# VectorE's loop turned so that it begins with a step's closing multiply, one product moved from step 0 to step 3, one transpose moved to the front of step 7

## What is computed

```python
x = x + L0(x, cond)   # attention over two keys: a fixed one and one made of cond
x = x + L1(x, cond)   # gated MLP, plus 8 experts with the top 2 chosen by a router
x = x + L2(cond, x)   # x @ W_e plus a row made of cond
x = x + L3(x, h0=cond)

def step(carry, xz_t):                      # L3, one position
    prev_h, prev_c = carry
    z = xz_t + prev_h @ Wh                  # 4 gates of 256, for 2 sequences
    ai, af, ao, ag = jnp.split(z, 4, axis=1)
    next_c = sigmoid(af) * prev_c + sigmoid(ai) * tanh(ag)
    next_h = sigmoid(ao) * tanh(next_c)
```

## Time and profile before

| | |
|---|---|
| median of 3 runs | 2004.42 us (2003.37 to 2004.9) |
| profiled execution | 2006.19 us, of it 2004.4 us span |
| TensorE busy | 1848.3 us (92%) |
| weight loads busy | 1462.6 us (73%) |
| VectorE busy | 1351.8 us (67%) |
| GpSimd busy | 1134.2 us (57%) |
| ScalarE busy | 812.2 us (41%) |
| DMA | 14.67 MB, mean 7 GB/s |

### The profile page before, as it was taken

One profiled execution on the slowest core, in us unless ns is written; L12 is line 12 of the kernel. 1 busy time (PEld: TensorE's weight loads), 2 busy tenths in 40 slices (PEclk: granted clock), 3 DMA queues, 4 the chain that ended last, 5 costly groups with the idle time before them and its releaser, 6 DMA issues. The chain is left out here.

```text
span 2004.4 us, 255266 instructions
## 1 busy us (share of the span) xinstructions
PE 1848.3 (92%) x113164; PEld 1462.6 (73%) x113164; DVE 1351.8 (67%) x7215; ACT 812.2 (41%) x4757; POOL 1134.2 (57%) x4950
## 2 busy tenths in 40 slices
PE   7899999999999999999999999999999999999998
PEld 5677777777777777777777777777777777777776
DVE  2566666666666666666666666666666666676666
ACT  2344444444444444444444444444444444444443
POOL 3555555555555555555555555555555555555555
PEclk9899999999999999999999999999999999999999
DMA  4000000000000000000000000000000000000000
GB/s 166 3 4 3 3 4 3 3 3 4 3 3 4 3 3 3 4 3 3 4 3 3 4 3 3 3 4 3 3 4 3 3 3 4 3 3 4 3 3 3
DMA packets 57724, 14.67 MB, mean 7 GB/s; under 512 B 56176, under 2 KB 56304, under 8 KB 57200
## 3 DMA queue, kind: packets, MB, share of 16 engines
q1 hardware_dynamic: 57712, 14.50, 3.1%
HBM read 12.37 MB, written 2.10 MB: 7 GB/s over the span
## 5 line engine op out<-in xcount | busy, mean ns | idle before, releaser
L916 PEld LDWEIGHTS psum<-wh_sb,h_ring 128*2 128x2 f32 (+1 forms) x32768 | 519.6, 90 | 446.0 <-DVE h_ring L740 414.9
L916 PE MATMUL psum<-wh_sb,h_ring 128*2 128x64 f32 (+1 forms) x32768 | 690.8, 219 | 138.7 <-DVE h_ring L740 121.4
L926 PE MATMUL psum<-h_ring,wh_sb 128*32 128x2 f32 x65536 | 768.7, 173 | 3.5 <-issue 3.5
L926 PEld LDWEIGHTS psum<-h_ring,wh_sb 128*32 128x32 f32 x65536 | 725.0, 109 | 13.3 <-issue 3.7
L517 ACT ACTIVATE f_act<-psum 128x4 f32<-128x4 f32 x1024 | 177.2, 173 | 763.7 <-DVE psum L711 755.1
L711 DVE STREAM_TRANSPOSE psum<-psum 128x64 f32<-128x64 f32 x1024 | 264.6, 258 | 306.6 <-PE psum L916 306.4
L789 PE MATMUL psum<-up_sb,x 128*32 128x512 f32 x2064 | 282.7, 605 | 0.0
L713 DVE STREAM_TRANSPOSE psum<-psum 128x64 f32<-128x64 f32 x1024 | 270.6, 264 | 16.1 <-PE psum L916 3.0
L795 PE MATMUL psum<-down_e,hid_t 128*16 128x256 f32 x3096 | 268.0, 381 | 0.6 <-ACT down_e L498 0.6
L723 DVE TENSOR_TENSOR_SCAN psum<-addend,psum 128x16 f32<-128x16 f32 x1024 | 199.2, 195 | 71.4 <-ACT psum L520 29.3
L740 DVE SCALAR_TENSOR_TENSOR h_ring<-o_act,psum 128x4 f32<-128x4 f32 x1024 | 163.0, 159 | 116.8 <-ACT psum L526 87.7
(11 more groups left out here) (141 smaller groups left out, 2224.7 us busy)
## 6 DMA issues: line engine op xcount, KB each, us to landing
x_a<-in_x SPq DMA_DIRECT2D x129, 16.0 KB, 1.6
x_s<-in_x SPq DMA_DIRECT2D x129, 16.0 KB, 1.7
up_sb<-in_up SPq DMA_DIRECT2D x1, 2048.0 KB, 12.6
out_y<-y_sb SPq DMA_DIRECT2D x128, 16.0 KB, 1.4
down_sb<-in_down SPq DMA_DIRECT2D x1, 1536.0 KB, 8.2
wx_sb<-in_wx SPq DMA_DIRECT2D x1, 1024.0 KB, 14.7
wh_sb<-in_wh SPq DMA_DIRECT2D x1, 1024.0 KB, 17.9
wkv_sb<-in_wkv SPq DMA_DIRECT2D x1, 512.0 KB, 4.2
```

Source lines behind the costliest of these rows:

```text
L916: last = nc.tensor.matmul(z[32 * j:32 * j + row + B, :], h_ring[:, prev, c, WIN - B - row:WIN], wh_v[:, c, g, j, :], start=False, stop=(c ...
L926: last = nc.tensor.matmul(by_row(z)[32 * j:32 * (j + 1), m, row:row + B], wh_v[:, c, g, j, 32 * m:32 * (m + 1)], h_ring[:, prev, c, WIN - ...
```

## The change

Three edits. First, VectorE's loop is turned by one instruction: the multiply that closes a step now stands at the start of the next step's code, so the close of step 7 is the first instruction of the next turn, behind the loop's branch, and the last close stands behind the loop. So that the first turn has something to close, `o_act` is set to 0 and `c_tanh` to 2 x cond ahead of the loop, which replaces the instruction that wrote the first hidden state. Second, `stream_mm(x1)` goes from step 0 to step 3 of the turn before, behind `attend`, and carries the count `x3_made` (its first instance stands ahead of the loop). Third, the transpose of `hid_s` in step 7 goes from behind the scan to ahead of the f transpose, with its wait for L598's result.

```diff
--- before.py
+++ after.py
@@ -543,10 +543,10 @@
             nc.vector.memset(partial_b, 0.0).then_inc(bank_clear, 1)
             nc.vector.memset(cell_all, 0.0).then_inc(bank_clear, 1)
             nc.vector.memset(addend[:, :], 1.0).then_inc(terms_set, 1)
+            nc.vector.memset(o_act[:, :], 0.0).then_inc(terms_set, 1)
 
             dve.wait_ge(cleared, 11)
             dve.wait_ge(small_in, 16)
-            nc.vector.tensor_scalar(h_ring[:, U - 1, :, WIN - B:WIN], cond, 2.0, None, ALU.mult).then_inc(hid, 1)
             dve.wait_ge(kv_made, 1)
             nc.vector.tensor_tensor(kv[:, :, :], bank[0][:, 0:2 * C * B].rearrange("p (m b) -> p m b", b=B),
                                     b_kv.unsqueeze(2).to_broadcast([P, 2 * C, B]), ALU.add).then_inc(kv_out, 1)
@@ -666,10 +666,13 @@
             hidden_a(2 * U)
             hidden_s(2 * U)
             dve.wait_ge(fold_out, BLOCKS)
-            dve.wait_ge(terms_set, 1)
+            dve.wait_ge(terms_set, 2)
             nc.vector.memset(factor, 0.0).then_inc(terms_set, 1)
-            dve.wait_ge(terms_set, 2)
+            dve.wait_ge(terms_set, 3)
             nc.vector.memset(factor_q[:, :, 3], 0.5).then_inc(terms_set, 1)
+
+            nc.vector.tensor_scalar(c_tanh.rearrange("p (c b) -> p c b", b=B), cond, 2.0, None,
+                                    ALU.mult).then_inc(terms_set, 1)
             dve.wait_ge(bias_scaled, 1)
             bias_x(READY)
             dve.wait_ge(x3_made, READY)
@@ -680,10 +683,24 @@
             invert_inv(2 * U)
             dve.wait_ge(x_injected, READY)
             base_f(READY + U)
-            dve.wait_ge(terms_set, 3)
+            dve.wait_ge(terms_set, 5)
+
+            def close(slot):
+
+                nc.vector.scalar_tensor_tensor(out=h_ring[:, slot, :, WIN - B:WIN],
+                                               in0=o_act[:, :].rearrange("p (c b) -> p c b", b=B), scalar=1.0,
+                                               in1=c_tanh.rearrange("p (c b) -> p c b", b=B),
+                                               op0=ALU.add, op1=ALU.mult).then_inc(hid, 1)
+
 
             with dve.Fori(READY, READY + T, U) as t:
+                now = t
                 for u in range(U):
+                    dve.wait_ge(cell_tanh, now)
+                    if u == 1:
+
+                        dve.wait_ge(h_read, now)
+                    close((u - 1) % U)
                     now = dve.snap(t + (u + 1))
                     if u == 0:
 
@@ -707,6 +724,8 @@
                     elif u == 7:
                         hidden_s(now)
                         invert_inv(now)
+                        dve.wait_ge(hid_s_out, now)
+                        turn(0, hid_s[:, :], hid_st, U)
                     dve.wait_ge(f_made, now)
                     nc.vector.transpose(t_f, z_f).then_inc(f_turned, 1)
                     dve.wait_ge(i_made, now)
@@ -730,17 +749,8 @@
                         bias_x(U)
                     elif u == 6:
                         hidden_a(now)
-                    elif u == 7:
-                        dve.wait_ge(hid_s_out, now)
-                        turn(0, hid_s[:, :], hid_st, U)
-                    dve.wait_ge(cell_tanh, now)
-                    if u == 0:
-
-                        dve.wait_ge(h_read, now)
-                    nc.vector.scalar_tensor_tensor(out=h_ring[:, u, :, WIN - B:WIN],
-                                                   in0=o_act[:, :].rearrange("p (c b) -> p c b", b=B), scalar=1.0,
-                                                   in1=c_tanh.rearrange("p (c b) -> p c b", b=B),
-                                                   op0=ALU.add, op1=ALU.mult).then_inc(hid, 1)
+            dve.wait_ge(cell_tanh, READY + T)
+            close(U - 1)
 
         @block.tensor
         def _(pe):
@@ -908,6 +918,7 @@
             inject().then_inc(x_injected, READY)
             pe.wait_ge(own_first, 2)
             attend(attn_b, w1_own[:, :])
+            stream_mm(x1)
             pe.wait_ge(wh_scaled, 2)
 
             def recur_row(z, g, row, prev):
@@ -947,7 +958,6 @@
                     if u == 0:
 
                         pe.wait_ge(hid_st, now)
-                        stream_mm(x1)
                         down_mm(0).then_inc(stream_made, U)
                     elif u == 1:
 
@@ -965,7 +975,8 @@
                         sum_mm()
                         pe.wait_ge(own_out, now)
 
-                        attend(attn_b, w1_own[:, :]).then_inc(x3_made, U)
+                        attend(attn_b, w1_own[:, :])
+                        stream_mm(x1).then_inc(x3_made, U)
                     elif u == 4:
                         up_mm(0, x1)
                     elif u == 5:
```

## The result

The changed kernel takes 1959.68 us (median of 4 runs, 1959.43 to 1960.97), the kernel before 2004.66 us (4 runs, 2003.37 to 2005.9): a ratio of 0.9777, 95% interval 0.976 to 0.9794.

What follows compares the result with a forecast made beforehand. Bound: the ring of waits in one recurrence step, not an engine. 0.20 + 0.10 - 0.02 - 0.01 = 0.27 us a turn, 34.6 over 128 turns, less 0.4, gives 1970.2 us; own range 1960 to 1980, 8 in 10 1959 to 1987.

Steps and rivals of the forecast that it cites:

- The loop turned: Step 0: the copy for the i gate starts 0.20 us earlier, gaining 0.20 us a turn, ends 0.14 and 0.24.
- The branch behind the scan: End of step 7: the wait for the cell's tanh covers the branch, cost 0, upper bound 0.05 us.
- The stream product out of step 0: Step 1: shorter fillers free the overwriting of x1 earlier, gaining 0.10 us a turn, ends 0.11 and 0.04.
- The stream product into step 3: Steps 3 and 4: TensorE's idle time covers the product, but L604 starts later; cost 0.02 us, ends 0 and 0.10.
- The rival with the passes one behind the other: Steps 3 and 4: the stream products run serially, delaying L604; net 0.16 us a turn slower, 2024 us, chance 0.03.
- The transpose in step 7: Step 7: hid_s's transpose ahead of the f transpose costs 0.01 us, ends 0 and 0.07.
- Ahead of the loop and in its first turns: Ahead of the loop: new instructions, with a multiply and a branch, cost 0.4 us once.
- The clock: TensorE: its clock should stay at the upper level because its idle stretches only get shorter.
- Slower, by the branch: Loop's branch, VectorE: the target must be loaded before the closing multiply, 1.2 us net a turn, about 2160 us, chance 0.02.

Runs made afterwards that it cites:

- e1: The kernel before with the loop turned and the transpose of hid_s moved, the stream product left in step 0: 1973.66 us.
- e5: The changed kernel with one more, long-met wait in front of the copy for the i gate in step 0: 1961.61 us.
- e3: The kernel before with only the transpose of hid_s moved ahead of step 7's f transpose: 2005.11 us.
- e4: The changed kernel with the transpose of hid_s put back behind the scan in step 7: 1966.36 us.
- e9: e2 with the stream product computed a second time in step 7, where it is not needed: 1991.98 us.
- e6: The changed kernel with the stream product computed twice in a row in step 3: 2005.78 us.
- e2: The kernel before with only the stream product moved from step 0 to step 3: 2066.5 us.
- e8: The changed kernel with the stream product in step 7 instead of step 3 and the up products spread over steps 3, 4 and 5: 2631.54 us.
- e11: The changed kernel with the stream product in step 7 instead of step 3 and attend's 8 small products computed again in step 7: 2130.55 us.
- e10: The changed kernel with the stream product in step 7, the first up product split over steps 3 and 4, the second whole in step 5: 1953.54 us.

## Why the prediction was right, and where it was off

The mechanism was right in each term of the sum; the sizes were off in one direction, by 11 us in all. What was said of the clock was wrong, and there the forecast was lucky.

- *The loop turned.* Forecast 0.20 with an upper end of 0.24; measured 0.24 (2.063 to 1.821, and 1.824 in e1). The step that was mis-sized is "the copy for the i gate follows the close directly, at 0.16 (its duration)". It follows at 0.075. So the last spread starts at 0.37 instead of 0.46, the c products at 0.65 instead of 0.74, and L520 at 1.21 instead of 1.25, where the i transpose sets it. The branch's real cost was 0.28 (0.36 less 0.075), and the 0.20 of idle time before the copy showed only the part beyond the close's end. This makes 0.04 a turn, 5 us, and is the largest of the errors. I guessed that e5 would explain the 0.075 by a missing wait, and it did not.
- *The branch behind the scan.* Taken at 0, measured at 0. That the third edit is what makes room for it is shown by the pair e3 and e4: nothing by itself, 5 to 7 us once the branch stands there. The prediction named no worth for it ("removed behind the scan it frees nothing"), which is true of the loop before and false of the turned one.
- *The stream product out of step 0.* Forecast 0.10, measured 0.108 (e9: the same).
- *The stream product into step 3.* I took 0.02 for L604 at 0.52; it came at 0.41 and cost nothing. About half of that is the start: the product began at -0.31 (1008.74 against the close at 1009.05), where I had it at -0.25. The other half is the time from there to L604, 0.72 instead of 0.77. Why it is shorter here than in step 0, where L588 starts 0.80 behind the first filler (1002.92 to 1003.72), is not shown. The rival with the passes one behind the other wanted 1.20 for it and is out. e6 shows that the cover I described as thin is real: past it, 0.43 us of chain cost 0.35.
- *The transpose in step 7.* 0.01 taken, 0.00 measured, partly by luck: I had the transpose of `hid_s` start at 0.50 and overlooked the reciprocal L585 in front of it. It started at 0.56 and left VectorE later than the f product came (the f transpose starts at 0.80), and nothing was lost only because the f transpose then took 0.22 instead of 0.27.
- *Ahead of the loop and in its first turns.* 0.4 us of loss taken; the span less 128 times 0.353 leaves 1.6 us won. That is no gain of the change: the first product of the recurrence starts anywhere from 41.1 to 42.9 us in the profiled executions of this study, at 42.2 before and at 41.2 after.
- *The clock.* "Its idle stretches only get shorter" was wrong as a reason. The second edit leaves TensorE idler around the turn's head: 0.81 us instead of 0.66 from the close of step 6 to the close of step 1, the difference in step 1, and 0.26 us fewer of weight loads in step 0. e2 fell to half its clock in one turn of five for that, 72 us. In the changed kernel the turned loop shortens the same stretch by 0.24 us and the clock stays at 1.00; that the one is the reason of the other is not shown, since 0.79 us of idle time are left there. So the second edit is worth 14 us behind the first (1973.7 to 1959.7) and costs 60 without it. No rival of mine had this, and the forecast was right here by luck: the edits came together, and its argument did not need that. The page "TensorE: Matmul & The Clock Gate" of the Trainium skill (Part 1) has the rule that the clock is set by how busy TensorE has been of late, with half of it when it was too idle; e2 and e9 agree with it (0.50 in one turn of five, and 1.00 once step 7 has work), and the changed kernel beside e2 is not explained by it from the records.
- *Slower, by the branch.* VectorE's branch never had to load code: the changed kernel has 9 packets of it, as the kernel before. But the mechanism exists in this kernel on the engine with the longest turn: e8 and e11. The page "Runtime: NRT & Kernel Launch" of the Trainium skill (Instruction fetch mechanics) has it that a taken branch whose target is not among the stored pages waits until that page is loaded; the trace agrees, with 352 and 135 packets of code against 9, and the long gaps at the loop's head.

## What to carry to other kernels

In a recurrence, read the time from one closing instruction to the next for each step of the loop: the steps that are longer than the shortest one name what can be won (read all of them: step 3 was left out here), and the loop's own branch is one of the things that belongs where an engine waits anyway. Before a filler is moved, compare its chain on the busiest column group with the idle time in its new place, since one chain fitted here for nothing and a second one cost 80% of its length. And check two things that no step's critical path shows: what the work left behind does to TensorE's clock, and whether the turn's code still fits, because the one turned an improvement of single steps into a loss of 60 us (e2), the other into one of 670 us (e8).

## What the runs showed of the hardware that was not expected

- Work that is not needed made a kernel 75 us faster (e2 to e9) by keeping TensorE's granted clock at 2.4 GHz. The clock had fallen with no gap on TensorE longer than 0.64 us ahead of it.
- TensorE's loop with 16 more matmul and 16 more weight-load records in a turn of 882 each loads program code again and again, but not in every turn (135 and 352 packets instead of 9, in 14 and 38 of the turns, gaps up to 5.5 us). With 8 more of each (e10) it does not.
- On VectorE a copy or transpose started 0.075 us behind the start of a 0.16 us multiply, before its end, and others at 0.167; a wait in between that was long met cost 0.004 (0.075 to 0.079, e5).
- A transpose that starts 0.05 late in the record ended on time (0.22 instead of 0.27 us, step 7), so a late start by itself need not be a loss.
